# A graph attention layer on one core: one stage with a running softmax per target in place of segment maximum and attention sum

## The chip, the cores and the metric

One core of a Trainium2 chip. The metric is the device time of one launch in microseconds, the lower the better. The kernel before takes 6463.39 us, the median of 3 runs (6460.63 to 6470.77).

## The reference

Four graph layers over 50,000 nodes and 25,000 edges, each followed by a residual and a layer norm. A node row has 160 numbers: 64 scalars and 32 vectors of 3. The edges are sorted by their target, `dst`. The change concerns the third layer, whose attention is, cut to what matters:

```python
a = jnp.einsum('ehk,hk->eh', _smooth_leaky(alpha), alpha_dot)     # 8 heads
amax = jax.ops.segment_max(a, edge_dst, num_segments=n)
a = jnp.exp(a - amax[edge_dst])
a = a / (jax.ops.segment_sum(a, edge_dst, num_segments=n)[edge_dst] + 1e-12)
ns = jax.ops.segment_sum(vs * a[..., None], edge_dst, num_segments=n)        # 64 numbers a node
nv = jax.ops.segment_sum(vv * a[..., None, None], edge_dst, num_segments=n)  # 96 numbers a node
```

So each target needs, for each of 8 heads, the largest score of its edges, the sum of the exponentials and the sum of the values weighted by them.

## The kernel before, in words

The work is cut into stages, each a block of five engine programs that ends in a barrier: `hidden_phase`, then for layers 0 and 1 `edge_phase_01` and a node stage, `edge_phase_23` for layer 2, `attention_max_phase`, `attention_sum_phase`, `node_phase_2`, `edge_phase_23` for layer 3, `node_phase_3`. An edge stage walks over NB = 49 blocks of B = 512 edges, which lie as T = 4 tiles of 128 edges, one edge a partition. A node stage walks over 98 blocks of 512 nodes.

Every engine's order is written out by hand: `pipeline` takes a list of (lag, step) and in step m of the loop runs each step for block m - lag, in the order of the list. Buffers come in rings of R = 4 (index r) or 2 (index u), and each step waits on semaphores whose counts are multiples of the block number. SP (SyncE) issues the plain loads and stores. GpSimd issues indirect DMAs, one for each tile: 128 rows of a table in HBM, the row numbers in SBUF.

Layer 2's edge stage leaves in `dram["val"]`, for each edge, 160 values (64 scalars, then 96 vector numbers) and 8 scores (line 1117 stores them, 336 KB a block).

`attention_max_phase` (1667) finds each target's largest scores. VectorE's `split` cuts each score in three bf16 pieces, TensorE's `turn_rows` (1873) turns them, ScalarE copies them (1859), SP lays them as rows `arow` (1753). TensorE's `spread` adds for each tile and head the 128 scores of the tile, spread over all partitions (1886), and -1e30 where the targets differ (1888, `apart`). VectorE's `largest` (1833) reduces 8 x 128 to 8. Table rows come in with `fetch` (1777) and go out with `send` (1784), 32 bytes each. There are four tables `mx`, one for each tile of a block. A tile's gather waits for the write that the same tile of the previous block made in the same table. In VectorE's order the tile's maximum with its table row (1842) is a step later than its reduction. Four tables are preset at the start (1730, 1.6 MB each) and merged at the end (1760 to 1762, 1851).

`attention_sum_phase` gathers each edge's maximum (`big`, 1956), takes the exponential of the difference (1978, 2002), weighs the values (1991), builds `same` (1985), which is 1 where two edges of a block have the same target, and sums over equal targets by 10 products of 128x128 with 128x168 in fp32 (2020; each fp32 product is two instructions in the trace). The sums are copied out (2007) and added to the table `agg[2]` by an accumulating indirect DMA (1966). The index `cidx` sends all but one edge of a target in a block to spare rows, so no row stands twice in one DMA. `cidx` is computed in the first edge stage (`targets`, 368 to 393): `product` (384) counts with an accumulator read how many earlier edges of the block have the same target. `node_phase_2` loads the table's rows, divides by the sum of exponentials (2459, 2545) and goes on.

Of the kernel before, what the change touches and what calls it, by code (L numbers as in the profile page):

```python
# [15 lines left out]
F32 = mybir.dt.float32  # L16
BF16 = mybir.dt.bfloat16
# [25 lines left out]
AW = {0: 161, 1: 161, 2: 168, 3: 192}  # L43
# [141 lines left out]
def edge_phase_01(nc, l, x, agg, dram, wt, later):  # L185
# [4 lines left out]
    with ExitStack() as ctx:  # L190
# [24 lines left out]
        if l == 0:  # L215
            product = sb("product", [P, T, B])
            cnt = sb("cnt", [P, T])
            away = sb("away", [P, T])

# [26 lines left out]
        idx_out = [sem(f"idx_out{r}") for r in range(R)]  # L246
        c_ps = sem("c_ps")
# [14 lines left out]
        def _(sp):  # L262
# [32 lines left out]
            sp.wait_ge(zset, 1)  # L295
            if l == 0:
                edge_pipeline(sp, ((0, load), (3, load_late), (7, keep_cidx), (7, clear_next)))
                for r in range(R):
                    sp.wait_ge(idx_out[r], 16 * ((NB - 1 - r) // R + 1))
# [6 lines left out]
        def _(pool):  # L306
# [25 lines left out]
            pool.memset(zero[:], 0.0).then_inc(zset, 1)  # L332
            edge_pipeline(pool, ((0, gather), (6, add)))
# [3 lines left out]
        def _(v):  # L337
# [23 lines left out]
            def targets(i, r, k, parts):  # L361
# [29 lines left out]
                v.wait_ge(idx_out[r], 16 * k)  # L391
# [603 lines left out]
def edge_phase_23(nc, l, x, agg, dram, wt, later, yn):  # L995
# [16 lines left out]
    with ExitStack() as ctx:  # L1012
# [26 lines left out]
        else:  # L1039
# [4 lines left out]
            val = [sb(f"val{u}", [P, T, W]) for u in range(2)]  # L1044
# [120 lines left out]
        def _(v):  # L1165
# [89 lines left out]
            def messages(i, r, k, parts):  # L1255
# [16 lines left out]
                if l == 2:  # L1272
# [4 lines left out]
                    v.tensor_tensor(val[u][:, :, 64:160], vec, m2[:], ALU.add).then_inc(val_ok, 1)  # L1277
# [13 lines left out]
        def _(a):  # L1291
# [28 lines left out]
            def silu(i, r, k, parts):  # L1320
# [5 lines left out]
                a.activation(val[u][:, :, 0:64], ob[u][:, :, SO + 64:SO + 128], ACT.Copy).then_inc(vs_ok, 1)  # L1326
# [340 lines left out]
def attention_max_phase(nc, dram, mx, wt):  # L1667
# [3 lines left out]
    HOME = (0, 1, 2, 1)  # L1671
    FREE = (4, 2, 4, 2)
    with ExitStack() as ctx:
        sb = lambda n, s, d=F32: ctx.enter_context(nc.sbuf_tensor(f"{n}_m", s, d))
        ps = lambda n, s: ctx.enter_context(nc.psum_tensor(f"{n}_m", s, F32))
        sem = semaphores(nc, ctx, lambda n: f"{n}_m")
        each = lambda count, f, n, *a: [f(f"{n}{q}", *a) for q in range(count)]
        tidx = each(R, sb, "tidx", [P, T], I32)
        gidx = each(R, sb, "gidx", [P, T], I32)
        trow = each(R, sb, "trow", [P, B], I32)  # L1680
        att = each(R, sb, "att", [P, T, H])
        three = each(2, sb, "three", [P, T, 3, H])
# [3 lines left out]
        ones = sb("ones", [P, P], BF16)  # L1686
# [1120 lines left out]
```

## Time and profile before

| | us |
|---|---|
| median of 3 runs | 6463.39 |
| the profiled execution | 6468.58 |
| its span, first to last instruction | 6466.8 |
| TensorE busy | 5101.9 (79%) |
| GpSimd busy | 4361.7 (67%) |
| VectorE busy | 4234.2 (65%) |
| ScalarE busy | 2848.6 (44%) |
| mean granted TensorE clock | 0.909 of full speed |

The shares of busy time are means over stages with different limits, so the stages are read one by one, from their windows. In the page, "idle before, releaser" is the time in which an engine stood still ahead of a group, with what ended the wait; "issue" is time in which the engine waited for nothing that the profile shows. Gathers are `out<-table,index`, writes `table<-tile,index`. The granted clock is a share of 2.4 GHz; the two levels are 1.2 and 2.4 GHz.

### The profile page before, as it was taken

What the parts mean: (1) busy time and instruction counts of PE and PEld (TensorE: products, weight loads), DVE (VectorE), ACT (ScalarE), POOL (GpSimd) and SP (SyncE); (2) the same over time, 40 slices, a digit from 0 to 9 for tenths busy, and PEclk for the clock granted to TensorE, in tenths of its full rate; (3) what the DMA queues carried; (4) which work ended last, traced back from release to release, by engine and by line L of the source; (5) the groups of instructions that cost most, each with busy time, mean ns of one, the idle gap of its engine ahead of it and who ended that gap; (6) DMA issues with size and microseconds to landing.
All of it is one profiled execution on the core that took longest, in us unless ns stands there. A gap on an engine that the chain in (4) does not pass through costs nothing. (4 is left out here: it accounts for less than half of the span.)

```text
span 6466.8 us, 123966 instructions
## 1 busy us (share of the span) xinstructions
PE 5101.9 (79%) x27989; PEld 3926.1 (61%) x28012; DVE 4234.2 (65%) x14730; ACT 2848.6 (44%) x6258; POOL 4361.7 (67%) x4641
## 2 busy tenths in 40 slices
PE   8889966679997886999655434338999989998776
PEld 6556656646666885767422134337888867776665
DVE  3566658854544786888677621216888878776788
ACT  5333347744443554444200000006777764443666
POOL 8688856658886877766277678875666657887222
PEclk9899989979998998999888766668999999999999
DMA  8566667736665663555311244443333325554665
GB/s 323 124 121 122 124 161 223 221 103 127 130 129 158 206 206 122 162 163 159 130 34 32 61 97 76 74 56 99 107 108 109 109 88 92 85 87 66 225 224 186
DMA packets 584565, 845.56 MB, mean 131 GB/s; under 512 B 216827, under 2 KB 334035, under 8 KB 579859
## 3 DMA queue, kind: packets, MB, share of 16 engines
q1 hardware_dynamic: 405587, 691.27, 33.5%
q0 software_dynamic: 178752, 151.88, 16.7%
q8 instruction: 68, 1.11, 0.1%
q14 instruction: 158, 1.29, 0.1%
HBM read 465.84 MB, written 375.78 MB: 130 GB/s over the span
## 5 line engine op out<-in xcount | busy, mean ns | idle before, releaser
L1143 POOL DMA_INDIRECT xg<-x,gidx x588 | 608.2, 1034 | 244.4 <-issue 181.1
L330 POOL DMA_INDIRECT agg<-summed,cidx x392 | 630.4, 1608 | 196.0 <-issue 111.5
L2020 PE MATMUL pc_a<-msg_a,same_a 128*128 128x168 f32 x980 | 258.1, 450 | 403.3 <-ACT summed_a L2007 346.4
L2020 PEld LDWEIGHTS pc_a<-msg_a,same_a 128*128 128x128 f32 x980 | 245.0, 305 | 416.9 <-issue 290.2
L403 DVE TENSOR_TENSOR pr<-pf,ws 128x512 f32<-128x512 f32 x196 | 135.6, 692 | 512.7 <-PE pf L490 395.6
L1154 POOL DMA_INDIRECT agg<-summed,cidx x196 | 317.5, 1620 | 78.2 <-issue 57.3
L1966 POOL DMA_INDIRECT agg<-summed_a,cidx_a x196 | 311.5, 1589 | 69.6 <-issue 58.5
L1317 ACT ACTIVATE ob<-po 128x416 f32<-128x416 f32 (+1 forms) x392 | 197.7, 504 | 354.0 <-PE po L1394 185.0
L1886 PE MATMUL pm_m<-arow_m,ones_m 128*128 128x512 bf16 x392 | 151.5, 477 | 227.6 <-DVE top_m L1833 225.3
L519 PEld LDWEIGHTS pc<-ob,same 128*128 128x128 f32 x1960 | 279.5, 194 | 83.4 <-issue 83.4
L2202 POOL TENSOR_TENSOR rs_n<-ve_n,wsb 128x4 f32<-128x4 f32 x98 | 98.7, 1007 | 338.0 <-DVE nm_n L2190 338.0
L2109 PE MATMUL pk_n<-wsb,xta_n 128*128 128x192 f32 x784 | 214.7, 356 | 121.2 <-ACT xtb_n L2124 121.2
L519 PE MATMUL pc<-ob,same 128*128 128x161 f32 x1960 | 303.4, 311 | 6.5 <-ACT summed L457 6.5
L1380 PE MATMUL ph<-esT,wsb 128*128 128x512 f32 x588 | 302.1, 595 | 2.3 <-DMA trow<-in_src_r 2.3
L625 PE MATMUL pk_n<-wsb,xta_n 128*128 128x160 f32 x784 | 190.2, 324 | 125.4 <-DVE y_n L680 112.6
L2007 ACT ACTIVATE summed_a<-pc_a 128x672 f32<-128x672 f32 x49 | 35.8, 731 | 561.1 <-DMA agg<-summed_a,cidx_a 559.0
L1252 DVE TENSOR_TENSOR pr<-pf,ws 128x512 f32<-128x512 f32 (+1 forms) x245 | 168.4, 687 | 150.8 <-PE pf L1368 83.9
L497 PE MATMUL ph<-hs,wsb 64*128 64x512 f32 x392 | 229.2, 666 | 47.9 <-ACT ws L444 45.5
L2556 POOL TENSOR_TENSOR rsa_n<-var_n,wsb 128x8 f32<-128x8 f32 x98 | 160.4, 1637 | 155.0 <-DVE var_n L2489 155.0
L1956 POOL DMA_INDIRECT big_a<-mx,tidx_a x196 | 197.1, 1006 | 92.0 <-issue 46.9
L1833 DVE TENSOR_REDUCE top_m<-pm_m 128x8 f32<-128x1024 f32 x196 | 238.7, 1221 | 24.6 <-PE pm_m L1888 24.1
L1303 ACT ACTIVATE ws<-ph 128x512 f32<-128x512 f32 x294 | 176.8, 601 | 171.2 <-PE ph L1380 166.9
(354 smaller groups left out, 17650.5 us busy)
## 6 DMA issues: line engine op xcount, KB each, us to landing
ar_n<-agg SPq DMA_DIRECT2D x194, 322.0 KB
agg<-zero SPq DMA_DIRECT2D x50, 768.0 KB
ar_n<-agg SPq DMA_DIRECT2D x97, 384.0 KB
agg<-zero SPq DMA_DIRECT2D x50, 672.0 KB
ar_n<-agg SPq DMA_DIRECT2D x97, 336.0 KB
agg<-zero_h SPq DMA_DIRECT2D x25, 1288.0 KB, 5.4
agg<-zero SPq DMA_DIRECT2D x50, 644.0 KB
x<-xn_n SPq DMA_DIRECT2D x97, 324.0 KB, 3.5
```

The costliest lines, as they stand in the source:

```text
L330: pool.indirect_dma_start(agg, bass.IndirectOffsetOnAxis(ap=cidx[r][:, t:t + 1], axis=0), summed[u][:, t, :], None, compute_op=ALU.add).th ...
L497: pe.matmul(ph[:], wt(f"w{g + 1}_{l}"), hs[NH - 1][:], start=True, stop=True).then_inc(w_ps, 1)
L519: last = pe.matmul(pc[:, t, 0:W], same[u][:, s, t * P:(t + 1) * P], ob[u][:, s, 32:32 + W], start=(s == t), stop=(s == T - 1))
L1143: pool.indirect_dma_start(xg[s][r][:, t, 0:XR], None, x, bass.IndirectOffsetOnAxis(ap=gidx[s][r][:, t:t + 1], axis=0)).then_inc(gathered[r ...
L1154: pool.indirect_dma_start(agg, bass.IndirectOffsetOnAxis(ap=cidx[r][:, t:t + 1], axis=0), summed[u][:, t, :], None, compute_op=ALU.add).th ...
L1317: a.activation(ob[u][:, t, :], po[:, t % 2, 0:TW], ACT.Copy).then_inc(ob_ok, 1)
L1380: pe.matmul(ph[:, (r + g) % 2 if l == 2 else 0], wt(f"w{g + 1}_{l}"), esT[r][:], start=True, stop=True).then_inc(w_ps, 1)
L1833: v.tensor_reduce(top[u][:, t, :], pm[HOME[t]][:], AX.X, ALU.max).then_inc(top_ok, 1)
L1956: pool.indirect_dma_start(big[r][:, t, :], None, mx, bass.IndirectOffsetOnAxis(ap=tidx[r][:, t:t + 1].bitcast(U32), axis=0)).then_inc(big_ ...
L1966: pool.indirect_dma_start(agg, bass.IndirectOffsetOnAxis(ap=cidx[r][:, t:t + 1], axis=0), summed[r % 2][:, t, :], None, compute_op=ALU.add ...
L2020: last = pe.matmul(pc[:, t, 0:W], same[u][:, s, t * P:(t + 1) * P], msg[u][:, s, :], start=(s == t), stop=(s == T - 1))
L2109: pe.matmul(pk[u][:, t, 0:192], xta[u][:, t * P:(t + 1) * P], wt("na_3"), start=True, stop=False)
```

## The change

One stage, `attention_phase`, takes the place of the two. The table `agg[2]` has 176 columns now: 8 heads of 21 (8 scalars, 12 vector numbers, the sum of exponentials) and 8 running maxima. For each block the stage takes the maximum over the block's own edges of a target (within each tile as before, then over the 4 tiles by 16 small products with `lone`, the tile maxima of those edges that are the first of their target in the tile), the exponentials and sums against that maximum, and then joins sums and table rows: the new maximum is the larger of both, and each side is scaled by the exponential of its maximum minus the new one. All four tiles' rows are gathered at once, joined at once and written at once, by plain writes. The masks are made by ScalarE: (difference of targets) squared is `far`, and Relu(1 - far) is `same`. `first` is computed in the first edge stage and stored with `cidx`. Blocks go through the steps with lags up to 8. In the diff below, most waits of the new steps are left out; those of SP, GpSimd and `rise` that order the work stand.

```diff
-AW = {0: 161, 1: 161, 2: 168, 3: 192}
+AW = {0: 161, 1: 161, 2: 176, 3: 192}
+VW = 168
...
@@ edge_phase_01, SP keep_cidx (l == 0) and GpSimd @@
+                sp.wait_ge(first_ok, i + 1)
+                fence(sp)
+                sp.dma_start(dram["first"][bass.ds(i, 1)].rearrange("a p t -> (a p) t"), first[r][:]).then_inc(idx_out[r], 16)
...
+            if l == 1:
+                pool.wait_ge(zset, 1)
+                pool.memset(zero[:].rearrange("p (r c) -> p r c", c=AW[2])[:, :, VW:AW[2]], -1e30).then_inc(zset, 1)
...
@@ edge_phase_01, VectorE targets (l == 0) @@
+                v.wait_ge(first_ok, i)
+                for t in range(T):
+                    m = t * P
+                    v.scalar_tensor_tensor(near[:, t, :], trow[r][:, m:m + P], tf[:, t:t + 1], wt("before")[:, t * B + m:t * B + m + P],
+                                           ALU.is_equal, ALU.mult, accum_out=ahead[:, t:t + 1]).then_inc(ahead_ok, 1)
...
+                v.wait_ge(ahead_ok, T * (i + 1))
+                v.tensor_scalar(first[r][:], ahead[:], 0.0, None, ALU.is_equal).then_inc(first_ok, 1)
...
@@ edge_phase_23, values by head @@
-                    v.tensor_tensor(val[u][:, :, 64:160], vec, m2[:], ALU.add).then_inc(val_ok, 1)
+                    v.tensor_tensor(val[u][:, :, 0:160].rearrange("p t (h k) -> p t h k", h=8)[:, :, :, 8:20], vec.rearrange("p t (h k) -> p t h k", h=8),
+                                    m2[:].rearrange("p t (h k) -> p t h k", h=8), ALU.add).then_inc(val_ok, 1)
...
-def attention_max_phase(nc, dram, mx, wt):
-def attention_sum_phase(nc, dram, mx, agg, wt):
+def attention_phase(nc, dram, table, wt):
...
@@ SP @@
+            def load_late(i, r, k, parts):
+                sp.wait_ge(msg_ok, due(i - 3))
+                sp.dma_start(val[r][:], dram["val"][bass.ds(i, 1)].rearrange("a p t c -> (a p) t c")).then_inc(late[r], 16)
+                sp.dma_start(first[r][:], dram["first"][bass.ds(i, 1)].rearrange("a p t -> (a p) t")).then_inc(late[r], 16)
+            def load_cidx(i, r, k, parts):
+                sp.wait_ge(sent, due(16 * T * (i - 3)))
+                sp.dma_start(cidx[r][:], dram["cidx"][bass.ds(i, 1)].rearrange("a p t -> (a p) t")).then_inc(cidx_in[r], 16)
+            long_pipeline(sp, ((3, to_row), (0, load), (3, load_late), (5, load_cidx)))
...
@@ GpSimd @@
+            def fetch(i, r, k, parts):
+                pool.wait_ge(cidx_in[r], 16 * (k + 1))
+                pool.wait_ge(sent, 16 * T * i)
+                for t in range(T):
+                    pool.indirect_dma_start(old[r][:, t, 0:W], None, table, bass.IndirectOffsetOnAxis(ap=cidx[r][:, t:t + 1], axis=0)).then_inc(old_in, 16)
             def send(i, r, k, parts):
+                pool.wait_ge(new_ok, i + 1)
+                for t in range(T):
+                    pool.indirect_dma_start(table, bass.IndirectOffsetOnAxis(ap=cidx[r][:, t:t + 1], axis=0), new[r % 2][:, t, :], None).then_inc(sent, 16)
+            long_pipeline(pool, ((8, fetch), (8, send)))
...
@@ VectorE (split as before, largest as before) @@
+            def once(i, r, k, parts):
+                v.tensor_tensor(lone[u][:], top[u][:], first[r][:].unsqueeze(2).to_broadcast([P, T, H + 1]), ALU.mult).then_inc(lone_ok, 1)
+            def biggest(i, r, k, parts):
+                v.tensor_scalar(miss[:], pg[:, :, :, H], -1.0, 1e30, ALU.add, ALU.mult).then_inc(big_ok, 1)
+                v.tensor_tensor(cand[:], pg[:, :, :, 0:H], miss[:].unsqueeze(3).to_broadcast([P, T, T, H]), ALU.add).then_inc(big_ok, 1)
+                v.tensor_reduce(old[r][:, :, W:W + H], cand[:].rearrange("p t s h -> p t h s"), AX.X, ALU.max).then_inc(big_ok, 1)
+                v.tensor_tensor(dif[r % 2][:], val[r][:, :, 160:168], old[r][:, :, W:W + H], ALU.subtract).then_inc(dif_ok, 1)
+            def weighted(i, r, k, parts):
+                v.tensor_tensor(m[:, :, :, 0:K], by_head(val[r][:, :, 0:160]), m[:, :, :, K:K + 1].to_broadcast([P, T, H, K]), ALU.mult).then_inc(msg_ok, 1)
+            def rise(i, r, k, parts):
+                v.wait_ge(old_in, 16 * T * (i + 1))
+                v.tensor_tensor(new[u][:, :, S:W], old[r][:, :, S:W], old[r][:, :, W:W + H], ALU.max).then_inc(nm_ok, 1)
+                v.tensor_tensor(gap[:], old[r][:, :, S:W + H].rearrange("p t (j h) -> p t j h", j=2),
+                                new[u][:, :, S:W].unsqueeze(2).to_broadcast([P, T, 2, H]), ALU.subtract).then_inc(gap_ok, 1)
+            def join(i, r, k, parts):
+                v.tensor_tensor(by_head(kept[:]), by_head(old[r][:, :, 0:S]), share[:, :, 0].unsqueeze(3).to_broadcast([P, T, H, K + 1]), ALU.mult).then_inc(part_ok, 1)
+                v.tensor_tensor(by_head(part[:]), by_head(sums[u][:]), share[:, :, 1].unsqueeze(3).to_broadcast([P, T, H, K + 1]), ALU.mult).then_inc(part_ok, 1)
+                v.tensor_tensor(new[u][:, :, 0:S], kept[:], part[:], ALU.add).then_inc(new_ok, 1)
+            long_pipeline(v, ((1, split), (4, largest(0)), (4, largest(1)), (5, biggest), (8, rise), (6, weighted), (8, join),
+                              (4, largest(2)), (4, largest(3)), (4, once)))
...
@@ ScalarE @@
+            def masks(i, r, k, parts):
+                a.activation(ntf[:], tidx[r][:], ACT.Copy, scale=-1.0).then_inc(ntf_ok, 1)
+                for t in range(T):
+                    a.activation(far[u][:, t, :], trow[r][:], ACT.Square, bias=ntf[:, t:t + 1], scale=1.0).then_inc(far_ok, 1)
+                a.activation(same[r][:], far[u][:], ACT.Relu, bias=one[:, 0:1], scale=-1.0).then_inc(same_ok, 1)
+            def shares(i, r, k, parts):
+                a.activation(share[:], gap[:], ACT.Exp, scale=0.8).then_inc(share_ok, 1)
+            long_pipeline(a, ((7, summed), (2, copied), (5, weights), (8, shares), (3, masks)))
...
@@ TensorE (spread as before, one step for each tile; add_up is the sum stage's product) @@
+            def across(i, r, k, parts):
+                for t in range(T):
+                    for s in range(T):
+                        last = pe.matmul(pg[:, t, s, 0:H + 1], same[r][:, s, t * P:(t + 1) * P], lone[u][:, s, :], start=True, stop=True)
+            long_pipeline(pe, ((4, spread(0)), (4, spread(1)), (5, across), (4, spread(2)), (6, add_up), (4, spread(3)), (2, turn_rows)))
...
@@ node_phase_2 @@
-                v.tensor_scalar(den[u][:], ar[r][:, :, 160:168], 1e-12, None, ALU.add).then_inc(den_ok, 1)
+                v.tensor_scalar(den[u][:], ar[r][:, :, 0:VW].rearrange("p t (h k) -> p t h k", h=H)[:, :, :, 20], 1e-12, None, ALU.add).then_inc(den_ok, 1)
```

## Rows read from the trace of the kernel before

**Rows 1.** Busy time of the engines by stage; (x) counts instructions. First edge, maximum, attention sum.

```profile
204.00:862.00 658.00, 594.50 (x2642) 392.77 (x2643) 416.80 (x1421) 228.82 (x440) 511.13 (x384) 0.93 0.63 120
3160.00:3724.00 564.00, 270.54 (x957) 110.44 (x980) 372.14 (x988) 28.76 (x49) 382.87 (x393) 0.77 0.23 56
3724.00:4375.00 651.00, 258.06 (x980) 245.04 (x980) 125.71 (x392) 43.21 (x99) 508.62 (x392) 0.64 0.44 73
```

**Rows 2.** Timeline, where the maximum stage begins.

```profile
3160.61 2.77 POOL L1767 MEMSET part_m<- 128x3200 f32 x1 [65.76 <-POOLq L131]
...
3182.26 0.18 DVE L1805 CAST piece_m<-att_m 128x32 bf16<-128x32 f32 x1 [16.65 <-DMA trow_m<-in_dst_r]
```

**Rows 3.** Timeline, where the attention sum ends and the node stage begins.

```profile
4367.38 1.55 POOL L1966 DMA_INDIRECT agg<-summed_a,cidx_a  x1 [0.30 <-issue]
4375.79 0.35 DVE L2443 TENSOR_SCALAR wsb<-wsb 64x256 f32<-64x256 f32 x1 [42.53 <-PEq L131]
```

**Rows 4.** Groups by form, GpSimd; busy, mean ns, idle before it.

```profile
L1966 POOL DMA_INDIRECT agg<-summed_a,cidx_a x196 | 311.5, 1589 | 69.6 <-issue 58.5 <-ACT summed_a L2007 8.4 <-DMA agg<-summed_a,cidx_a 2.7
...
L315 POOL DMA_INDIRECT xg<-x,gidx x196 | 194.3, 991 | 64.3 <-issue 60.5 <-DMA ea<-in_ea 1.7 <-ACT summed L457 0.9
L1784 POOL DMA_INDIRECT mx<-new_m,gidx_m x196 | 192.0, 980 | 62.1 <-issue 46.8 <-DVE new_m L1842 15.3
...
L1777 POOL DMA_INDIRECT old_m<-mx,gidx_m x196 | 188.1, 960 | 93.2 <-issue 55.1 <-DMA gidx_m<-in_dst_t 32.1 <-DVE new_m L1842 3.9
```

**Rows 5.** Timeline: last gather of a group, and the VectorE instruction waiting for it.

```profile
3692.66 0.95 POOL L1777 DMA_INDIRECT old_m<-mx,gidx_m  x1 [0.30 <-issue]
...
3695.49 0.17 DVE L1842 TENSOR_TENSOR new_m<-top_m,old_m 128x8 f32<-128x8 f32 x1 [1.38 <-DMA old_m<-mx,gidx_m]
```

**Rows 6.** The same pair in the middle of the attention sum.

```profile
3910.05 0.94 POOL L1956 DMA_INDIRECT big_a<-mx,tidx_a  x1 [0.30 <-issue]
...
3914.70 0.19 DVE L1978 TENSOR_TENSOR dif_a<-val_a,big_a 128x32 f32<-128x32 f32 x1 [5.31 <-DMA big_a<-mx,tidx_a]
```

**Rows 7.** Tile view of new_m: write to landing.

```profile
DMA to landing us min/median/max: 2.1/2.1/2.1
```

**Rows 8.** Timeline, GpSimd alone: accumulating writes, and one that awaits their landing.

```profile
831.60 1.56 POOL L330 DMA_INDIRECT agg<-summed,cidx  x1 [0.30 <-issue]
835.89 1.67 POOL L330 DMA_INDIRECT agg<-summed,cidx  x1 [2.73 <-DMA agg<-summed,cidx]
```

**Rows 9.** Tile view of top_m: duration min/median/max, first and last start.

```profile
L1833 DVE TENSOR_REDUCE top_m<-pm_m x196: 1209/1224/1226, 3190.4 to 3685.7; 128x8 f32<-128x1024 f32 x196
```

**Rows 10.** Groups by form, VectorE, the widest elementwise operation.

```profile
L2171 DVE TENSOR_TENSOR y_n<-sg_n,xr_n 128x640 f32<-128x640 f32 x98 | 80.9, 826 | 10.9
```

**Rows 11.** Timeline: one block of the attention sum's products, granted clock 0.64.

```profile
3921.18 5.25 PE L2020 MATMUL pc_a<-msg_a,same_a 128*128 128x168 f32 x20 [7.92 <-ACT summed_a L2007]
```

**Rows 12.** Timeline: a block's segment products of the first edge stage.

```profile
571.81 3.00 PE L519 MATMUL pc<-ob,same 128*128 128x161 f32 x20
```

**Rows 13.** Timeline: eight products of two columns, full clock.

```profile
105.93 1.84 PE L1543 MATMUL pv_h<-wsb,sq_h 128*128 128x2 f32 x16
```

**Rows 14.** Timeline: products of one tile in the maximum stage, either clock.

```profile
3406.08 0.59 PE L1886 MATMUL pm_m<-arow_m,ones_m 128*128 128x512 bf16 x2 [4.72 <-DVE top_m L1833]
...
3407.98 1.06 PE L1886 MATMUL pm_m<-arow_m,ones_m 128*128 128x512 bf16 x2
```

**Rows 15.** Timeline of ScalarE after the attention sum.

```profile
4401.19 0.52 ACT L2399 ACTIVATE sq_n<-x_n 128x384 f32<-128x384 f32 x1 [3.25 <-DVE x_n L2471]
4401.73 1.28 ACT L2418 ACT_TABLE_LOAD   x1
```

**Rows 16.** VectorE by form, in 400 to 800 us of the first edge stage.

```profile
L403 DVE TENSOR_TENSOR pr<-pf,ws 128x512 f32<-128x512 f32 x60 | 41.5, 692 | 131.0 <-ACT ws L444 89.6 <-PE pf L490 40.8
...
L384 DVE SCALAR_TENSOR_TENSOR product<-trow,tf,wsb 128x128 f32<-128x128 int32 x30 | 10.2, 341 | 0.0
...
L384 DVE DVE_READ_ACCUMULATOR product<-trow,tf,wsb 128x1 f32 x120 | 9.4, 79 | 0.0
```

More of the change, by code:

```diff
@@ L218, in edge_phase_01 @@
             away = sb("away", [P, T])
+            ahead = sb("ahead", [P, T])
+            near = sb("near", [P, T, P])
+            first = [sb(f"first{r}", [P, T]) for r in range(R)]
         pt = ps("pt", [P, 2, B])
@@ L1043, in edge_phase_23 @@
             sm = sb("sm", [P, T, 64])
-            val = [sb(f"val{u}", [P, T, W]) for u in range(2)]
+            val = [sb(f"val{u}", [P, T, VW]) for u in range(2)]
             zero = sb("zero", [P, ZS * AW[3]])
@@ L1686, in attention_max_phase @@
         ones = sb("ones", [P, P], BF16)
+        one = sb("one", [P, 1])
         arow = each(2, sb, "arow", [P, H, B], BF16)
         diag = sb("diag", [P, 4, P], BF16)
-        part = each(T, sb, "part", [P, NA // P * H])
-        tf = sb("tf", [P, T])
-        apart = each(2, sb, "apart", [P, T, P], BF16)
-        top = each(2, sb, "top", [P, T, H])
-        old = each(2, sb, "old", [P, T, H])
-        new = each(2, sb, "new", [P, T, H])
+        ntf = sb("ntf", [P, T])
+        far = each(2, sb, "far", [P, T, B], BF16)
+        same = each(R, sb, "same", [P, T, B])
+        top = each(2, sb, "top", [P, T, H + 1])
+        lone = each(2, sb, "lone", [P, T, H + 1])
+        miss = sb("miss", [P, T, T])
+        cand = sb("cand", [P, T, T, H])
+        dif = each(2, sb, "dif", [P, T, H])
+        msg = each(2, sb, "msg", [P, T, S])
+        sums = each(2, sb, "sums", [P, T, S])
+        old = each(R, sb, "old", [P, T, W + H])
+        new = each(2, sb, "new", [P, T, W])
+        gap = sb("gap", [P, T, 2, H])
+        share = sb("share", [P, T, 2, H])
+        kept = sb("kept", [P, T, S])
+        part = sb("part", [P, T, S])
         pa = ps("pa", [3 * H, B])
-        pm = each(3, ps, "pm", [P, H, P])
-        l_set = sem("l_set")
+        pm = each(2, ps, "pm", [P, H, P])
+        pg = ps("pg", [P, T, T, 16])
+        pc = ps("pc", [P, T, 256])
         blank = sem("blank")
-        l_out = sem("l_out")
         diag_ok = sem("diag_ok")
@@ L1845, in _ @@
[L1845 to L1851 removed]
+            def once(i, r, k, parts):
+                u = r % 2
+                v.wait_ge(top_ok, T * (i + 1))
+                v.wait_ge(late[r], 32 * (k + 1))
+                v.wait_ge(g_ps, due(i - 1))
+                v.tensor_tensor(lone[u][:], top[u][:], first[r][:].unsqueeze(2).to_broadcast([P, T, H + 1]), ALU.mult).then_inc(lone_ok, 1)
@@ L1874, in turn_rows, with spread, f @@
                 last.then_inc(turned, 1)
-            def spread(i, r, k, parts):
-                u = r % 2
-                pe.wait_ge(row_in[u], 16 * (2 * k + r // 2 + 1))
-                pe.wait_ge(ap_ok, T * (i + 1))
-                for t in range(T):
-                    n = HOME[t]
-                    pe.wait_ge(top_ok, due(T * i + t - FREE[t] + 1))
+            def spread(t):
+                def f(i, r, k, parts):
+                    u = r % 2
+                    if t == 0:
+                        pe.wait_ge(row_in[u], 16 * (2 * k + r // 2 + 1))
+                        pe.wait_ge(far_ok, T * (i + 1))
+                    pe.wait_ge(top_ok, due(T * i + t - 1))
@@ L2604, in build @@
         dram["cidx"] = nc.dram_tensor("cidx", (NBP, P, T), U32, kind="Internal").ap()
+        dram["first"] = nc.dram_tensor("first", (NB, P, T), F32, kind="Internal").ap()
         dram["hid"] = table("hid", NBH * 64, B)
         dram["hid3"] = table("hid3", NBH * 64, B)
-        dram["val"] = nc.dram_tensor("val", (NB, P, T, AW[2]), F32, kind="Internal").ap()
-        mx = [table(f"mx{u}", NA, 8) for u in range(T)]
+        dram["val"] = nc.dram_tensor("val", (NB, P, T, VW), F32, kind="Internal").ap()
         with nc.Block() as block:
```

296 lines of the change are left out of this document (104 added, 192 removed).

## The prediction, made before the change was run

> **What bounds the kernel now.** I read the page first: no engine is busy over 79% of the span, and each stage ends behind a barrier, so a stage is priced by itself. The windows view shows the two stages that are replaced: 564 us of maximum and 651 us of attention sum, 49 blocks each; GpSimd is the busiest engine in both, at 383 and 509 us [rows 1]. Its busy time is indirect DMAs: the groups by form give a mean of 0.96 to 0.99 us for a gather and 0.98 us for a plain write, 1.59 us for an accumulating write, and each is preceded by 0.30 us of issue [rows 4]. Eight in the maximum stage make 8 x 1.27 = 10.2 us a block. The first and the last of its 196 reductions start at 3190.4 and 3685.7 us [rows 9], which is 10.16 us a block: GpSimd never waits there. In the sum four gathers and four accumulating writes make 4 x 1.3 + 4 x 1.89 = 12.8 us of the 13.3 us that 651 / 49 gives. So both stages are bound by GpSimd's issuing, and landings are hidden: each tile of the maximum stage has a table of its own, and the sum gathers ahead of its writes. From the maximum stage's first instruction, 3160.6 us [rows 2], to the node stage's first, 4375.8 us [rows 3], there are 1215 us.
>
> **What the new stage must do in turn.** GpSimd issues 8 indirect DMAs a block in place of 16: 4 gathers of table rows, 4 plain writes. But the gather of block i waits for every write of block i-1 to land, and the writes need the gathers to have landed and VectorE to have joined. Nothing of GpSimd's overlaps within this ring, so I add it up:
> - Four gathers: 3 x (0.96 + 0.30) + 0.96 = 4.74 us [rows 4]. The row is 704 bytes where the maximum's was 32, but the gathers of 644-byte node rows have a mean of 0.99 us, so width costs a gather nothing.
> - Landing, until VectorE starts: 1.9 us. Rows 5 show 3695.49 - 3693.61 = 1.88 us on quiet queues, rows 6 show 3914.70 - 3910.99 = 3.71 us. In the latter SP had just issued 592 KB of target rows and values. In the new code the target rows (256 KB) are issued as the gathers begin, and the values (336 KB) wait for a message count that arrives after the gathers land. So I take the quiet value and keep 3.7.
> - `rise`, two small VectorE operations: 0.43 us (0.19 us is the small one in [rows 6], the second twice as wide and dependent). Then `weighted`, which stands ahead of `join` in VectorE's order: 640 elements, 0.80 us net of overlap, by 0.83 us for one of 640 [rows 10]. ScalarE's `shares` runs under it.
> - `join`: three operations of 672 elements, 0.86 us each by the same row, the first two overlapping: 2.5 us.
> - Hop and issue on GpSimd 0.45 us, four writes 3 x 1.28 + 0.98 = 4.82 us [rows 4].
> - Landing of the last write until the next gather starts. The tile view gives 2.1 us from issue to landing for a 32-byte row [rows 7], so 2.1 - 0.98 + 0.30 = 1.4 us at least; an accumulating write of 644 bytes leaves GpSimd idle for 2.73 us [rows 8]. The new write is plain like the one and wide like the other: 2.15 us, the middle; both ends kept.
>
> Sum: 4.74 + 1.9 + 0.43 + 0.80 + 2.5 + 0.45 + 4.82 + 2.15 = **17.8 us a block**.
>
> Rows 5 and 7 already hold the completion cost by which the ring lives. The Trainium skill, "DMA: Bandwidth & Descriptors", section "Anatomy of one DMA", puts it at about 2.0 us per DMA from GpSimd, whatever it moves, plus size over 436 GB/s. By that, 2.2 us from issue in both places where I have 2.9 and 3.1, the ring would be an estimated 16.2 us. The trace's 1.88 us behind the end of the instruction is the larger and is what I use.
>
> **The other ring.** TensorE and VectorE hand work to and fro: `weighted`, `add_up`, `spread` of tile 3, reduction 3, `once`, `spread` of tile 1, `across`, `biggest`, and `rise` again. With TensorE at 2.4 GHz: add_up 3.0 us [rows 12], spread 2 x 1.0 us (two pairs of 0.59 us that overlap) [rows 14], reduction 1.22 us [rows 9], across 16 products of nine columns, by the eight of two columns in 1.84 us [rows 13] 3.7 us; weighted, rise, once, the four small operations of `biggest` and hops 3 us: about 12.8 us. Shorter than 17.8, so it is cover, with 5 us to spare. At 1.2 GHz it is add_up 5.25 us, of a stretch at a granted mean of 0.64 [rows 1, 11], spread 2 x 1.9 [rows 14], across 7.4, the rest as before: 20.4 us. Then it would bound. The two old stages had means of 0.77 and 0.64 with TensorE busy 48% and 40% of the time; now both works meet in one stage and `across` is new, which makes 11 of 17.8 us at full clock. I take a mean over 0.8.
>
> VectorE's own sum is 4 x 1.22 + 7 x 0.18 for the split, and 6 for the rest: about 12 us of 17.8. ScalarE takes the masks: four squares of 512 columns, near 0.65 us each by the 0.52 us of a 384-column one [rows 15], a Relu of 2048 columns at about 2 us, and 2 us of small ones: 6.7 us, behind `shares` in its order and needed a step later, hidden. Square in an Exp stage needs no table load: rows 15 show it running on the set that the Exp stage left, and the load of 1.28 us coming only for the Silu after it. The Trainium skill, "ScalarE: Activation LUTs", section "Table sets: the hidden batching unit", tells to batch by set and names Relu but not Square among the functions that every set holds; by that rule the stage could reload twice a block, and the trace speaks against it.
> SP's loads, one to three steps ahead, wait for counts of earlier steps: nothing.
>
> **Stage total.** Fill: the presets of four tables go, for which the first VectorE split waited 16.65 us [rows 2]; about 13 of them are saved, so the first reduction comes near 3177 instead of 3190 us. Then one step of 7 us and three of the compute ring, 14 each, give `rise` of block 0 at 3226, 65 us after the start. 48 rings x 17.8 = 854 us. The last block: 0.43 + 0.80 + 2.5 + 0.45 + 4.82 + 1.3 = 10.3 us, and 5 us from there to the node stage (6.9 now, landing included [rows 3]). Also gone: the merge of four tables at the maximum's end, inside the 1215. 65 + 854 + 10 + 5 = 935, against 1215: **280 us less**.
>
> **Edits elsewhere.** First edge stage: four more products of 128 columns with their accumulator reads, 4 x (0.34 + 0.08), and a small one, 1.8 us a block on VectorE. It waits 131.0 / 30 = 4.4 us a block before its product `pr` [rows 16], and GpSimd with 16 DMAs' worth of busy and issue time bounds that stage (511 us busy of 658 [rows 1], and 384 x 0.30 of issue). Cost 0 to 90 us; I take 2, for the last blocks, where gathers no longer lead. One more 2 KB DMA a block: nothing. The wider preset of the second stage, values written and read in runs of 8 and 12, table rows 5% longer: same element counts, hidden DMAs, 1 us. Together +3.
>
> The profiled execution took 6468.6 us, with 6466.8 us of span: 6468.6 - 280 + 3 = 6191.6. The median of the runs shown is 5.2 us lower: **6186 us**.
>
> **Rivals.**
> - *Late landings.* Table rows 22 times as wide share the queues with SP's loads. Gather landing 3.7 [rows 6] and write gap 2.73 [rows 8]: ring 20.2 us, 6303. For it: the sum stage's crowd. Against: the loads' places in the new order.
> - *Wide writes cost as much as accumulating ones.* Nothing shows whether 1.59 us in [rows 4] is the adding or the width. Four times 0.61: ring 20.2, 6305. Against: gathers don't care for width.
> - *Half clock.* TensorE waits some 4 us a block for `weighted`, and waits of 4.72 and 7.92 us stand ahead of products that ran slowly or before a mix [rows 11, 14]. Ring 20.4 us, 6311.
> - *Shorter ring.* Both landings at their lower ends and joins overlapping better: 16.3 us, 6111.
> - *Slower.* The landing of the gather: it doubled from 1.88 to 3.71 us under load [rows 5, 6]; if wide rows at random addresses doubled it again, to 7.4, with the write gap at 2.73, the ring is 23.9 us and the kernel takes 6480. It decides from 23.6 us a block. For it: the ring exposes every landing, 98 of them, where before almost none was. Against: four gathers move only 360 KB.
> - *No gain by the first edge stage*: VectorE's 90 us on the path beside a ring of 21.6; nearly equal times.
>
> **How the numbers follow.** Forecast 0.53, late landings 0.12, wide writes 0.10, half clock 0.08, shorter 0.10, slower 0.05, no change 0.02. The range goes from the shorter ring, 6115, to just past the three at 20.2 to 20.4, 6320. A measurement of this kernel tells 0.2%, 13 us, from no change; all cases but the last two lie beyond it: faster 0.93, same 0.02, slower 0.05.
>
> **What would show it.** Right: 392 indirect DMAs of about 1 us in the one stage, their period 17.8 us, GpSimd near 44% busy, VectorE's `rise` waiting for the gather, GpSimd's first gather waiting for the write's landing, granted clock over 0.8, one table load. Wrong: plain writes at 1.6 us; `rise` starting at once after `biggest`; products of 128 columns at the lower clock; a first edge stage longer by over 5 us; a period under 16.

## The result, and the profile after

The changed kernel took **6554.66 us** (median of 3 runs, 6551.92 to 6563.73) against 6463.39 us: a ratio of 1.0144, 95% interval 1.013 to 1.0157. It is slower by 91 us. The forecast was 6186 us with a range to 6320, and 0.05 for slower.

The page of the changed kernel, its first lines and the slices:

```profile
span 6550.0 us, 126024 instructions
...
PE 5344.2 (82%) x29580; PEld 4138.0 (63%) x29580; DVE 4313.6 (66%) x14877; ACT 3077.9 (47%) x6601; POOL 3845.4 (59%) x4249
...
POOL 8678856558886887664122332235666657887222
PEclk9899989989998998999666666668999999999899
```

GpSimd's row falls to 1 to 3 tenths in slices 20 to 27, the new stage: nothing is left that keeps it busy. The granted clock is 0.6 there. The windows view of the new stage (3120 to 4460 us; engines in the order PE, PEld, DVE, ACT, POOL, then granted clock, DMA share, GB/s), which answers to [rows 1]:

```profile
3120.00:4460.00 1340.00, 777.04 (x3528) 574.47 (x3528) 523.72 (x1086) 303.03 (x491) 380.51 (x392) 0.67 0.19 51
```

GpSimd's busy time is less than half of what the two old stages had (380 us against 383 + 509), as forecast; no engine is over 58%; and the stage is longer. The timeline gives its ends and the tile view of new_a its rhythm (min/median/max ns, first and last start of VectorE's `rise`), in the places of [rows 2, 3, 9]:

```profile
3124.52 1.76 DVE L1831 MEMSET arow_a<- 128x2048 uint32 x1 [7.83 <-PEq L132]
...
4462.06 0.34 DVE L2425 TENSOR_SCALAR wsb<-wsb 64x256 f32<-64x256 f32 x1 [12.83 <-PEq L132]
```

```profile
L1897 DVE TENSOR_TENSOR new_a<-old_a x49: 186/193/194, 3215.4 to 4445.9; 128x32 f32<-128x32 f32 x49
```

From 3124.5 to 4462.1 are 1337.5 us, where the old stages took 1215.2: **122 us more**, not 280 less. Forty-eight periods between 3215.4 and 4445.9 make 25.63 us a block. The groups of GpSimd, beside [rows 4]:

```profile
L1823 POOL DMA_INDIRECT agg<-new_a,cidx_a x196 | 192.4, 982 | 729.7 <-DVE new_a L1910 684.9 <-issue 44.8
...
L1817 POOL DMA_INDIRECT old_a<-agg,cidx_a x196 | 188.1, 960 | 286.5 <-DMA agg<-new_a,cidx_a 134.2 <-DMA cidx_a<-cidx 101.7 <-issue 50.6
```

Neither a gather nor a plain write became dearer: 960 and 982 ns, with rows 22 times as wide. The time is in the 685 us for which the writes wait for `join`. One block of the timeline, from one `rise` to the next, the lines that make the chain:

```profile
3776.90 0.19 DVE L1897 TENSOR_TENSOR new_a<-old_a 128x32 f32<-128x32 f32 x1 [5.39 <-DMA old_a<-agg,cidx_a]
...
3777.27 0.82 DVE L1891 TENSOR_TENSOR msg_a<-val_a,msg_a 128x640 f32<-128x640 f32 x1
...
3778.14 5.75 PE L2002 MATMUL pc_a<-msg_a,same_a 128*128 128x168 f32 x20 [6.18 <-DVE msg_a L1891]
...
3784.59 0.60 PE L1966 MATMUL pa_a<-wsb,three_a 128*24 128x128 f32 x4
3785.23 0.59 ACT L1921 ACTIVATE attT_a<-pa_a 24x512 bf16<-24x512 f32 x1 [20.53 <-PE pa_a L1966]
3785.72 0.25 ACT L1941 ACTIVATE msg_a<-dif_a 128x32 f32<-128x32 f32 x1
3785.84 0.24 ACT L1951 ACTIVATE share_a<-gap_a 128x64 f32<-128x64 f32 x1
...
3786.11 0.86 DVE L1907 TENSOR_TENSOR kept_a<-old_a,share_a 128x672 f32<-128x672 f32 x1 [8.03 <-ACT share_a L1951]
...
3789.49 1.00 POOL L1823 DMA_INDIRECT agg<-new_a,cidx_a  x1 [14.29 <-DVE new_a L1910]
...
3796.97 0.99 POOL L1817 DMA_INDIRECT old_a<-agg,cidx_a  x1 [2.64 <-DMA agg<-new_a,cidx_a]
...
3803.33 0.19 DVE L1897 TENSOR_TENSOR new_a<-old_a 128x32 f32<-128x32 f32 x1 [5.11 <-DMA old_a<-agg,cidx_a]
```

Read it backwards from `join` (L1907). It waits 8.03 us for `shares` (L1951). That needs nothing but the gap, ready at 3777.34, and runs at 3785.84, because ScalarE runs its instructions in order and stands at `copied` (L1921), waiting 20.53 us for TensorE's `turn_rows` (L1966). `turn_rows` is the last stage in TensorE's order, behind `add_up` (L2002, 5.75 us) and the spread of tile 3, and `add_up` waits for the `weighted` (L1891) of this same step. So a preparation for a block six steps later, which nobody needs yet, sits between `rise` and `join` of the block at hand. The waits view over 3250 to 4350 us (total, times, longest):

```profile
ACT attT_a L1921 <- PE pa_a L1966: 835.0, 41, 21.9
POOL agg L1823 <- DVE new_a L1910: 586.5, 42, 14.9
DVE kept_a L1907 <- ACT share_a L1951: 325.2, 42, 8.6
```

325.2 / 42 = 7.7 us a block, nearly the whole excess of 25.63 over the 17.8 forecast.

**One stage outside the change moved too.** The node stage after the second edge stage, whose text is the same, takes from its first transpose to the first instruction of the next stage 443 us where it took 483. In the kernel before, VectorE's `y_n` starts late once in every 38 to 40 us, after nothing that the profile shows. Waits view and timeline of the kernel before, and the waits view of the changed one:

```profile
DVE y_n L910 <- issue: 52.9, 10, 12.2
```

```profile
2183.38 1.26 DVE L910 SCALAR_TENSOR_TENSOR y_n<-pk_n,a_n,xr_n 128x160 f32<-128x160 f32 x4 [4.66 <-issue]
...
2221.38 1.26 DVE L910 SCALAR_TENSOR_TENSOR y_n<-pk_n,a_n,xr_n 128x160 f32<-128x160 f32 x4 [4.84 <-issue]
```

```profile
DVE y_n L929 <- issue: 11.9, 1, 11.9
```

Ten idle times became one; the nine that went were 52.9 - 12.2 = 41 us. So the balance of the two traces is: all that comes before this stage +5, this stage -40, new stage +122, the rest -4, together the 83 us between the spans.

### The profile page after: what moved, and what is told of

It is laid out like the page before. It is cut to its first block and busy times, and to the rows that moved or that the text cites. A ratio compares the mean times of both kernels' runs of the same rounds, so it can differ in the third digit from the quotient of the medians.

```text
span 6550.0 us, 126024 instructions
## 1 busy us (share of the span) xinstructions
PE 5344.2 (82%) x29580; PEld 4138.0 (63%) x29580; DVE 4313.6 (66%) x14877; ACT 3077.9 (47%) x6601; POOL 3845.4 (59%) x4249
## 5 line engine op out<-in xcount | busy, mean ns | idle before, releaser
L1823 POOL DMA_INDIRECT agg<-new_a,cidx_a x196 | 192.4, 982 | 729.7 <-DVE new_a L1910 684.9
L2002 PE MATMUL pc_a<-msg_a,same_a 128*128 128x168 f32 x980 | 262.5, 456 | 274.9 <-DVE msg_a L1891 274.9
L1921 ACT ACTIVATE attT_a<-pa_a 24x512 bf16<-24x512 f32 x49 | 28.7, 586 | 934.9 <-PE pa_a L1966 934.9
L2002 PEld LDWEIGHTS pc_a<-msg_a,same_a 128*128 128x128 f32 x980 | 248.2, 309 | 317.8 <-DVE msg_a L1891 259.3
L1817 POOL DMA_INDIRECT old_a<-agg,cidx_a x196 | 188.1, 960 | 286.5 <-DMA agg<-new_a,cidx_a 134.2
L1979 PE MATMUL pm_a<-arow_a,ones_a 128*128 128x512 bf16 x392 | 169.9, 528 | 226.5 <-DVE top_a L1863 207.6
L1907 DVE TENSOR_TENSOR kept_a<-old_a,share_a 128x672 f32<-128x672 f32 x49 | 42.0, 858 | 333.0 <-ACT share_a L1951 333.0
L1863 DVE TENSOR_REDUCE top_a<-pm_a 128x8 f32<-128x1024 f32 x196 | 232.7, 1219 | 35.0 <-PE pm_a L1981 34.4
```

The lines of the kernel that those rows point to most:

```text
L1823: pool.indirect_dma_start(table, bass.IndirectOffsetOnAxis(ap=cidx[r][:, t:t + 1], axis=0), new[r % 2][:, t, :], None).then_inc(sent, 16)
L1863: v.tensor_reduce(top[u][:, t, 0:H], pm[t % 2][:], AX.X, ALU.max).then_inc(top_ok, 1)
L2002: last = pe.matmul(pc[:, t, 0:S], same[r][:, s, t * P:(t + 1) * P], msg[u][:, s, :], start=(s == t), stop=(s == T - 1))
```

## Experiments: who stands between rise and join

All are compared with the kernel before, run beside them on the same chip (its median 6468.8 us beside the first four, which ran on another chip than the others, 6463.3 and 6463.8 beside those). The first four kept the changed kernel and altered only the order of stages on one engine. Theory 1: ScalarE's head of line, as read above. Rivals: the late gather landing, TensorE's lower clock, and other rings that would hold the period up anyway.

**e1**, ScalarE's `copied` last:

```diff
-            long_pipeline(a, ((7, summed), (2, copied), (5, weights), (8, shares), (3, masks)))
+            long_pipeline(a, ((7, summed), (5, weights), (8, shares), (3, masks), (2, copied)))
```

> Only ScalarE's order in the new stage is changed: the copy of the turned scores stands last instead of second. Theory 1, ScalarE's queue: the shares stand behind that copy, which waits for TensorE's turning, which stands behind the segment products, which wait for the weighted values of the same step. VectorE's join then waits 7.7 us a block. With the copy last that wait goes, and the ring of table rows is left at the durations the changed kernel's trace gives: 0.9 hop, 4.8 writes, 2.9 to the gather, 4.75 gathers, 1.7 landing, 1.2 rise and weights, 2.5 join, together 18.7 us a block. 6210 us, between 6190 and 6250. Theory 2, clock: the products at a granted clock of 0.67 bound the stage, and ScalarE's wait is where the slack shows. Then the order changes little: 6500 to 6555.

Measured: **6197.2 us** (6192.7 to 6199.1), ratio 0.9582 (0.9566 to 0.9598). One reordered tuple gives back 357 us (363 by the ratios). The granted clock is 0.69 over 3250 to 3900 us, hardly above the 0.67 of the changed kernel, so the low clock alone did not hold the stage up. Its timeline:

```profile
3602.16 0.19 DVE L1897 TENSOR_TENSOR new_a<-old_a 128x32 f32<-128x32 f32 x1 [2.81 <-DMA old_a<-agg,cidx_a]
...
3602.65 0.26 ACT L1951 ACTIVATE share_a<-gap_a 128x64 f32<-128x64 f32 x1 [2.99 <-DVE gap_a L1899]
...
3603.27 0.85 DVE L1907 TENSOR_TENSOR kept_a<-old_a,share_a 128x672 f32<-128x672 f32 x1
...
3606.65 1.00 POOL L1823 DMA_INDIRECT agg<-new_a,cidx_a  x1 [6.28 <-DVE new_a L1910]
...
3610.52 0.97 POOL L1823 DMA_INDIRECT agg<-new_a,cidx_a  x1 [0.30 <-issue]
...
3613.70 0.99 POOL L1817 DMA_INDIRECT old_a<-agg,cidx_a  x1 [2.22 <-DMA agg<-new_a,cidx_a]
...
3614.37 0.33 SPq L1790 DMA_DIRECT2D val_a<-val  x1
...
3617.52 0.95 POOL L1817 DMA_INDIRECT old_a<-agg,cidx_a  x1 [0.30 <-issue]
...
3620.20 0.19 DVE L1897 TENSOR_TENSOR new_a<-old_a 128x32 f32<-128x32 f32 x1 [2.87 <-DMA old_a<-agg,cidx_a]
```

`shares` now waits for the gap alone, and `join` starts behind `weighted` without a wait. The ring is that of the forecast: 4.49 us from `rise` to the first write, 4.84 of writes, 2.21 of gap, 4.77 of gathers, 1.73 of landing, 18.04 us. The mean period is (4081.8 - 3195.3) / 48 = 18.47 us.

**e3**, the same wait attacked from TensorE's side: `turn_rows` ahead of `add_up`, ScalarE as in the changed kernel.

```diff
-            long_pipeline(pe, ((4, spread(0)), (4, spread(1)), (5, across), (4, spread(2)), (6, add_up), (4, spread(3)), (2, turn_rows)))
+            long_pipeline(pe, ((4, spread(0)), (4, spread(1)), (5, across), (4, spread(2)), (2, turn_rows), (6, add_up), (4, spread(3))))
```

> ScalarE's order as in the changed kernel; TensorE turns the scores ahead of the segment products instead of behind the last spread. Theory 1: the copy is then ready before the rise and ScalarE's queue is free: the same as with the copy last, 6190 to 6260. If some other thing than the chain over TensorE's turning holds the shares, nothing moves: over 6500.

Measured: 6209.2 us (6202.8 to 6223.8), ratio 0.9607 (0.9591 to 0.9623), period 18.51 us. Its clock was 0.74 over 3250 to 3900 us. Two repairs that share nothing but the supposed cause bring the same; with that the cause is shown.

**e2**, `shares` ahead of `copied`, but `masks` still behind it: ((7, summed), (5, weights), (8, shares), (2, copied), (3, masks)).

> ScalarE's order: the small exponentials (weights, shares) ahead of the copy, the masks behind it as in the changed kernel. Theory 1: the join no longer waits, but the masks start only after TensorE's turning, so the next spread waits for them; that ring is near 19 us. 6220 to 6270. If the shares alone are the cause, it equals the run with the copy last. Theory 2: 6500 to 6555.

Measured: 6317.5 us (6314.8 to 6321.0), ratio 0.9766 (0.975 to 0.9782), period 20.64 us. The direction was right and the size a miss by some 50 us. Its waits over 3250 to 3900 us show the same fault one place further on: `masks` stands behind the late `copied`, and the next step's spread of tile 0 waits for its squares.

```profile
ACT attT_a L1921 <- PE pa_a L1966: 215.7, 31, 8.1
...
PE pm_a L1979 <- ACT far_a L1932: 90.8, 25, 3.8
...
DVE new_a L1897 <- DMA old_a<-agg,cidx_a: 3.2, 2, 2.5
```

`rise` no longer waits for gathers (3.2 us in all): the table ring is not the longest there, the ring through the masks is.

**e4**, e1 with `join` ahead of `weighted` in VectorE's order, so that the table's ring is shorter by `weighted` and the ring of products longer by `join`:

```diff
-(5, biggest), (8, rise), (6, weighted), (8, join),
+(5, biggest), (8, rise), (8, join), (6, weighted),
```

> As the run with the copy last, and VectorE joins ahead of weighing the next values. If the ring of table rows bounds once the queue is free, it is 0.8 us a block shorter and the kernel some 35 us faster than that run, near 6175. If the ring of products and reductions bounds, weighing 2.5 us later lengthens it: 6260 to 6330. Theory 2: over 6550.

Measured: 6239.5 us (6237.6 to 6245.2), ratio 0.965 (0.9633 to 0.9666), 42 us above e1, period 19.38 us: neither figure expected. VectorE's wait for spread products rose from 92.9 us in 35 waits to 172.9 in 33, as it must when `weighted` comes later. But the ring of products is not what holds the period: `rise` still waits for its gathers in every block. Waits over 3250 to 3900 us, and one block of the timeline:

```profile
DVE new_a L1897 <- DMA old_a<-agg,cidx_a: 52.1, 33, 2.9
```

```profile
3609.97 0.19 DVE L1897 TENSOR_TENSOR new_a<-old_a 128x32 f32<-128x32 f32 x1 [1.54 <-DMA old_a<-agg,cidx_a]
...
3614.13 1.00 POOL L1823 DMA_INDIRECT agg<-new_a,cidx_a  x1 [7.77 <-DVE new_a L1910]
...
3624.74 0.33 SPq L1790 DMA_DIRECT2D val_a<-val  x1
3625.02 0.95 POOL L1817 DMA_INDIRECT old_a<-agg,cidx_a  x1 [0.30 <-issue]
...
3629.56 0.19 DVE L1897 TENSOR_TENSOR new_a<-old_a 128x32 f32<-128x32 f32 x1 [1.59 <-DMA old_a<-agg,cidx_a]
```

The first write comes 4.16 us after `rise`, 0.33 earlier than in e1; writes and gap are as there; but the landing after the last gather is 3.59 us in place of 1.73. What differs beside it is SP's load of the values (336 KB): with `weighted`, TensorE's work and so `turn_rows` and `copied` come later, SP's `to_row` waits for that and stands ahead of its loads, and SP reaches this load 0.28 us before the last gather, in e1 3.15 us before it. That is the "late landings" rival, here as the price of a reordering. Means over the 43 blocks of each timeline in which values are still loaded:

| run | values' load ahead of the last gather | landing after the last gather |
|---|---|---|
| changed kernel | 10.4 us | 1.65 us |
| e3 | 5.5 us | 1.69 us |
| e1 | 3.9 us | 1.76 us |
| e8 | 2.7 us | 1.94 us |
| e9 | 2.5 us | 2.12 us |
| e4 | 0.4 us | 3.39 us |

No run moved the load by itself, so the collision is read from the traces and not shown by an experiment. The margin of the ring of products is how long `rise` waits for gathers: 115.4 / 36 = 3.2 us a block in e1 and 52.1 / 33 = 1.6 in e4.

**e7**, both repairs at once.

> The changed kernel with both repairs at once: ScalarE's copied last, and TensorE's turn_rows ahead of add_up. Each alone brought 6197 and 6209 us. Theory 1 (with either, shares waits for nothing any more and the ring over the table's rows is what is left, 18.04 us in the block read): nothing more is gained, 6190 to 6212 us, period of rise 18.4 to 18.6 us. Theory 2 (TensorE's order still costs in the run with copied last): 6165 to 6185 us, period 17.9 to 18.2 us.

Measured: 6182.1 us (6179.1 to 6194.2), ratio 0.9561 (0.9545 to 0.9577), which overlaps e1's interval; period (4084.1 - 3197.9) / 48 = 18.46 us, as in e1. The two signs disagree: the period is that of theory 1, the median lies in the range of theory 2. The traced execution is the slowest of the four (6194.2 us; the others took 6179 to 6185), so its period says nothing of the faster three. Whether the second repair adds some 10 us stays open; that it adds little is shown.

## Experiments: what is left, and a faster version

**e8**, e1 with the join cut in two, so that GpSimd writes tiles 0 and 1 while VectorE joins 2 and 3:

```diff
-                v.tensor_tensor(by_head(kept[:]), ...
+                for n in range(2):
+                    h = slice(2 * n, 2 * n + 2)
+                    v.tensor_tensor(by_head(kept[:, h]), ...
...
+                    if t % 2 == 0:
+                        pool.wait_ge(new_ok, 2 * i + 1 + t // 2)
```

> The changed kernel with copied last on ScalarE, and the join of table rows cut in two: VectorE joins two of the four tiles, GpSimd writes these while VectorE joins the other two. Theory 1 (the ring over the table's rows sets the period: rise, shares, join 2.5 us, four writes, gap, four gathers, landing): the first write starts about 1.2 us earlier in every block, less some 0.2 us for three more instructions on VectorE, so 49 x 1.0 = 50 us less than with copied last alone, 6150 us (6140 to 6165). Theory 2 (the ring of the products and reductions is as long, as the run with the join first on VectorE suggested): most of it is not to be had, 6175 to 6200 us, and VectorE's waits for pm_a grow as rise's wait for old_a shrinks.

Measured: **6131.3 us** (6127.4 to 6136.4), ratio 0.9484 (0.9469 to 0.95). Period (4024.2 - 3195.6) / 48 = 17.26 us, 1.21 below e1's (by the ratios some 60 us less in all); the first write starts 3.42 us after `rise` in place of 4.49. The gain is larger than expected, the time 9 us under the range of theory 1: `fetch` also waits less for the writes to land, 84.2 / 38 = 2.2 us against 84.3 / 35 = 2.4.

**e9**, the same in four parts.

> As the join in halves, cut in four: VectorE joins one tile at a time and GpSimd writes it. With halves the period of rise was 17.26 us and the steps of the ring in the block read added up to 17.11 us (3.42 from rise to the first write, 4.84 of writes, 2.22 of gap, 4.76 of gathers, 1.87 of landing). Theory 1 (that ring alone is left): the first write starts some 0.6 us earlier, period 16.6 to 16.75 us, time 6100 us (6090 to 6115). Theory 2 (VectorE, with six more instructions in a block, or TensorE's products are as long by now): 6120 to 6150 us, waits of VectorE for pm_a grow and rise's wait for old_a is near nothing.

Measured: 6133.0 us (6125.0 to 6137.1), ratio 0.9486 (0.947 to 0.9502), the same as halves; period (4022.4 - 3197.7) / 48 = 17.18 us. The time fell where theory 2 put it, but not for its reason: VectorE's waits for spread products fell (58.9 us against 81.6 with halves) and `rise` still waits for its gathers (76.3 against 76.7). The timeline, GpSimd's first and second write and VectorE's joins between them:

```profile
3613.87 0.33 DVE L1909 TENSOR_TENSOR kept_a<-old_a,share_a 128x168 f32<-128x168 f32 x1
3613.96 1.11 POOL L1823 DMA_INDIRECT agg<-new_a,cidx_a  x1 [4.91 <-DVE new_a L1912]
...
3615.38 1.15 POOL L1823 DMA_INDIRECT agg<-new_a,cidx_a  x1 [0.31 <-issue]
...
3616.83 0.97 POOL L1823 DMA_INDIRECT agg<-new_a,cidx_a  x1 [0.30 <-issue]
```

The first write comes 2.91 us after `rise`, 0.51 earlier than with halves; two of the writes then take 1.11 and 1.15 us in place of 0.97 to 1.00, the four together 5.12 in place of 4.84, and the landing 2.00 in place of 1.87. Most of the gain went back there. This is one block; over 3250 to 3900 us GpSimd is busy 303.6 us for 302 DMAs where it was 293.5 for 303, which is 0.27 us a block more and fits.

**e10**, e8 with `add_up` cut to its four products on the diagonal, of ten: sums over targets that two tiles of a block share are left out.

> The join in halves with add_up cut to the four products on the diagonal, 4 of 10: the sums over the targets that two tiles of a block share are left out. Theory 1 (the ring over the table's rows alone sets the period with halves): no gain in the steady state, 6120 to 6135 us, although TensorE has some 3 us less to do in a block. Theory 2 (TensorE's work is part of the period, in each block or in many): the period falls under 17.0 us and the time under 6115 us.

Measured: 6133.9 us (6129.6 to 6143.5), ratio 0.9491 (0.9475 to 0.9507), period (4028.7 - 3195.5) / 48 = 17.36 us. Waits and windows over 3250 to 3900 us of e10, then the windows of e8:

```profile
DVE new_a L1898 <- DMA old_a<-agg,cidx_a: 166.1, 37, 6.4
```

```profile
3250.00:3900.00 650.00, 420.85 (x2278) 301.12 (x2277) 414.04 (x944) 240.84 (x376) 291.59 (x301) 0.70 0.30 80
```

```profile
3250.00:3900.00 650.00, 538.53 (x2730) 421.23 (x2729) 408.42 (x942) 241.20 (x376) 293.51 (x303) 0.70 0.29 80
```

TensorE has 118 us less to do in these 650 and nothing is won; `rise` just waits 166 us for its gathers in place of 77. With halves the ring over the table's rows sets the period, and TensorE, at 83% busy and a clock of 0.70, is cover.

## Experiments: the 40 us of an untouched stage

**e5**, the kernel before with the first-edge table alone: computed and stored in the first edge stage, read by nobody.

```diff
+                for t in range(T):
+                    m = t * P
+                    v.scalar_tensor_tensor(near[:, t, :], trow[r][:, m:m + P], tf[:, t:t + 1], ...
...
+                v.tensor_scalar(first[r][:], ahead[:], 0.0, None, ALU.is_equal).then_inc(first_ok, 1)
```

> The kernel before with one part of the change: the first edge stage also computes and stores the table of first edges, which nothing reads. Theory 1 (the 41 us that the node stage after the second edge stage lost in the changed kernel come from where VectorE's instructions of that stage lie, since nine idle times of 4.1 to 5.1 us before its y_n, one per turn of its loop and after nothing that the profile shows, are gone there and its text is the same): the extra instructions of the first edge stage move that loop too, the nine idle times go, and the time is 6468 + 5 - 41 = 6430 us (6420 to 6440). Theory 2 (they went with something else of the change: the wider table of that stage's neighbour, its blank columns, the later stage): they stay, and the time is the kernel before and the first stage's own cost of 4 to 6 us, 6465 to 6478 us.

Measured: 6427.6 us (6425.6 to 6430.6), ratio 0.9943 (0.9927 to 0.996).

**e6**, the kernel before with sixteen idle memsets ahead of VectorE's loop in that stage:

```diff
+            for n in range(16):
+                v.memset(pad[:, n:n + 1], 0.0)
```

> The kernel before with sixteen memsets of one column each, of a tile that nothing reads, ahead of VectorE's loop in that same node stage: they move the loop by sixteen instructions and cost about a microsecond. Theory 1 (position alone): if sixteen instructions are a shift that matters, the nine idle times before y_n go or change, and the time is 6425 to 6435 us. Theory 2: the idle times stay as they are, and the time is 6463 to 6474 us; then either position is not the cause or this shift is too small, and the run of the first-edge table decides.

Measured: **6422.6 us** (6420.2 to 6424.3), ratio 0.9933 (0.9917 to 0.995). Waits views of e5 and e6:

```profile
DVE y_n L924 <- issue: 13.2, 1, 13.2
```

```profile
DVE y_n L913 <- issue: 11.9, 1, 11.9
```

In both the nine idle times are gone. Sixteen instructions that do nothing make the old kernel 41 us faster (2 us more than the range of theory 1 allowed). The two edits lie in different stages and share, as far as the diffs show, only that more VectorE instructions stand ahead of this loop, so that the place of VectorE's code decides is well supported; a shift of its timing against the other engines was not tested apart, and what makes one place bad is not shown. The first edge stage's own cost is then 41 - 35.8 = 5 us by the medians, an estimate: from the stage's first preset to the end of its last accumulating write the traces show 681.1 us before, 682.8 in e5 and 685.2 in the changed kernel.

Against a kernel before without those idle times, 6423 us, the changed kernel is 132 us slower and e8 291 us faster.

## Why the prediction was wrong

**The step that failed** is in the ring's sum: "ScalarE's `shares` runs under it", priced at nothing. For `shares` alone the cover holds: in e1 its 0.26 us lie under `weighted`'s 0.82. But I costed the instruction and not the queue it stands in. In ScalarE's order `copied` is ahead of it; I listed ScalarE's work as 6.7 us "behind `shares` in its order" and never asked what `copied` waits for. The answer stood in the diff: `turn_rows`, last on TensorE, behind `add_up`. It measured 7.7 us a block in the waits view, and 25.63 - 18.47 = 7.16 us a block by its removal.

**The sum, redone.** The stage was put at 935 us and took 1337.5. The ring accounts for 48 x (25.63 - 17.8) = 376 us, the fill for 26 (first `rise` 90.9 us after the stage's start, 65 forecast; 68.6 in e1, so it is mostly the same cause), the end for 1. With +2 more in the first edge stage and -40 in the node stage, 6186 + 403 + 2 - 40 = 6551 us, against 6554.66 measured.

**Terms of the ring**, forecast against the block of the changed kernel and e1's: rise to first write 4.18 / 12.59 / 4.49; writes 4.82 / 4.84 / 4.84; gap 2.15 / 2.64 / 2.21; gathers 4.74 / 4.76 / 4.77; landing 1.9 / 1.60 / 1.73. All but one were good to 0.5 us. The hop from `join` to the first write was 0.87 us where I took 0.45. The mean wait for the writes to land was 118.5 / 41 = 2.9 us in the changed kernel and 84.3 / 35 = 2.4 in e1: nearer to the accumulating 2.73 [rows 8] than to the 1.4 that the narrow write gives [rows 7].

**The other ring** was called cover with 5 us to spare at a granted clock over 0.8. The clock was 0.67, and between 0.68 and 0.74 in the steady part of every variant; there `add_up` took 5.75 us, not 3.0. In e1 `rise` waited 3.2 us a block for its gathers, so this ring took about 18.5 - 3.2 = 15.3 us, not 12.8, and it stayed cover. The sum at 1.2 GHz throughout stayed a rival and did not come true (its terms as listed add up to 20.7 us, not 20.4). But the clock has a part in the loss, since `add_up` lay between `rise` and `join`: by an estimate from its two durations up to 5.75 - 3.0 = 2.7 of the 7.7 us. It was not tried.

**Right:** 392 indirect DMAs of about 1 us; a wide plain write costs no more than a narrow one (982 ns, against 1.6 us in that rival); gathers land soon in the changed kernel (1.60 us, against the 3.71 and 7.4 of two rivals), though not for the reason given: the values' load does not wait until the gathers have landed, it is issued before them (3791.04 against 3796.97), and in e1 among them; no second table load for Square. VectorE's addition to the first edge stage measured 4 x (0.348 + 0.079) = 1.7 us a block, and its wait before `pr` shrank from 131.0 us [rows 16] to 97.6 over the same 30 blocks: hidden as said, 5 us in all where I took 2. Wrong beside the ring: GpSimd was busy for 28% of the stage, not 44, and the clock was under 0.8.

On the estimate beside the ring: by the Trainium skill, "DMA: Bandwidth & Descriptors", section "Anatomy of one DMA", gather and write would each land about 2.2 us after their issue. Measured in e1 it was 2.68 us for the last gather (3617.52 to `rise` at 3620.20) and 3.18 us for the last write (3610.52 to 3613.70), both taken to the start of the instruction that waits, so the page's figure is low here by a half and by one us; with it the ring would come out 1.5 us short.

**The "slower" rival** had the right sign at 0.05 and the wrong mechanism. Nothing doubled; a queue was overlooked. As repaired in e1, the change lands at 6197 us, 11 from the forecast, but that is luck in part: without the 40 us that I did not foresee it would be 6237, 51 above.

## What to carry to other kernels

In a pipeline written as an order of stages per engine, walk each engine's list for every instruction on the critical ring: whatever is listed ahead of it can put its own wait on the ring, however late its result is needed. Put the stages that only prepare later blocks last, or start them early on the engine that feeds them; moving one entry was worth 357 us here, more than the change was meant to bring. And when a ring through DMA is the bound, cut its compute step so that the first transfer starts sooner (halves: some 60 us); cutting finer brought nothing here. A reordering that looks shorter on paper also moves the loads: look where they fall against the transfers of the ring (e4).

## What was not expected of the hardware

- A loop of VectorE can lose 4 to 5 us per turn to nothing the profile names, and be rid of it with sixteen more instructions ahead of the loop (52.9 us in 10 waits before, 11.9 in one after). A comparison of two kernels by under 1% should look for such `issue` waits first.
- GpSimd's plain indirect write of 128 rows took 0.98 us with 32-byte rows and with 704-byte rows alike; the gather took 0.96 us with both.
- Indirect writes issued while VectorE was joining took 1.11 and 1.15 us instead of 0.97 (e9).
- How long the last gather took to land went with the place of a plain load of 336 KB: 1.65 to 1.76 us on the mean with the load issued 3.9 us or more ahead of that gather, 3.39 us with the two issued almost together (e4). Single blocks of one kernel show it too: in e8 1.89 us at 2.75 ahead and 3.35 at 1.39.
- The granted clock of the new stage did not follow TensorE's load: 0.70 both at 539 and at 421 us busy of 650 (e8, e10), 0.67 in the changed kernel at 58% busy. It is a mean between the levels of 1.2 and 2.4 GHz in all of them.
